# An order of units for each engine in the last two layers, and the output projection between two tiles of keys

## The reference

```
# third layer, x already normalised to xn
Q, K, V = split(xn @ W_in.T + b_in)
Q, K = rope(Q), rope(K)
A = sum over tokens of (K / |K|) * V
x = x + (A * Q) @ W_out.T + b_out + xn
# fourth layer, x normalised again to xn
hidden = sigmoid(xn @ ternary(w1).T) * (xn @ ternary(w2).T)
x = x + hidden @ ternary(w3).T
```

## Time and profile before

| what | us |
|---|---|
| median of 3 runs (lowest, highest) | 691.55 (690.04, 693.25) |
| the profiled execution, its time | 693.51 |
| its span in the profile | 691.7 |
| first combine of the last two layers starts at | 501.29 |
| the five steps with all five streams | 538.61 to 640.76 |
| last add of the last batch starts at | 688.35 |

### The profile page before, as it was taken

One profiled execution on the slowest core, in us unless ns is written; L12 is line 12 of the kernel. 1 busy time (PEld: TensorE's weight loads), 2 busy tenths in 40 slices (PEclk: granted clock), 3 DMA queues, 4 the chain that ended last, 5 costly groups with the idle time before them and its releaser, 6 DMA issues.

```text
span 691.7 us, 10447 instructions
## 1 busy us (share of the span) xinstructions
PE 529.4 (77%) x3558; PEld 429.6 (62%) x3558; DVE 404.3 (58%) x981; ACT 294.5 (43%) x617; POOL 281.5 (41%) x417
## 2 busy tenths in 40 slices
PE   3275878888898888888656569999246898888976
PEld 2143555656565665657445469899234888888876
DVE  2453455756676766665255358886146676776653
ACT  2405455563636464642411147555133443354432
POOL 3606060645536262620232423343366566544110
PEclk9656979998899999998986689999768999999998
DMA  8500000020200000100100383444611011100000
GB/s 318 211 0 18 2 16 16 2 62 2 60 2 32 17 33 16 33 17 16 31 31 1 91 292 99 112 115 108 206 46 31 31 46 46 47 17 1 16 16 30
DMA packets 31347, 39.56 MB, mean 57 GB/s; under 512 B 9632, under 2 KB 27552, under 8 KB 30400
## 3 DMA queue, kind: packets, MB, share of 16 engines
q1 hardware_dynamic: 26016, 25.31, 11.0%
q0 software_dynamic: 4432, 9.33, 5.3%
q10 hardware_dynamic: 848, 4.26, 1.6%
HBM read 27.25 MB, written 11.51 MB: 56 GB/s over the span
## 4 chain that ended last, share of the span: by engine, by line
PE 49%; DVE 19%; ACT 12%; DMA 7%; POOL 6%; issue 5%; ACTq 1%; another core or an unknown queue 1%; SPq 0%; DVEq 0%; POOLq 0%
PE bank_c L1390 5%; PE bank_s L1290 4%; DVE nmx L959 4%; ACT pT L738 3%; PE bank_p L1290 3%; PE bank_s L1421 3%; PE bank_c L1372 3%; PE bank_g L1294 2%; PE bank_c L1294 2%; DMA tb_x<-row_ids 2%; PE bank_g L1296 2%; PE bank_c L1676 2%; PE bank_g L1295 2%; PE bank_c L1296 2%; PE bank_c L1295 2%
## 5 line engine op out<-in xcount | busy, mean ns | idle before, releaser
L738 ACT ACTIVATE pT<-bank_s 128x512 f32<-128x512 f32 x128 | 69.5, 595 | 41.9 <-PE bank_s L1421 41.4
L959 DVE TENSOR_REDUCE nmx<-bank_c 128x2 f32<-128x512 f32 x80 | 55.1, 688 | 45.3 <-PE bank_c L1390 38.4
L492 POOL TENSOR_TENSOR rt<-raw,rope_sb 128x384 f32<-128x384 f32 x16 | 16.0, 1001 | 119.8 <-ACT raw L677 106.6
L593 POOL DMA_INDIRECT xt<-h_rows,tb_x x39 | 37.3, 955 | 66.1 <-DMA tb_x<-row_ids 53.0
L1390 PE MATMUL bank_c<-kT,qT 64*128 64x256 f32 x160 | 43.3, 353 | 24.8 <-DVE nmx L959 20.1
L1390 PEld LDWEIGHTS bank_c<-kT,qT 64*128 64x128 f32 x160 | 25.9, 203 | 49.6 <-DVE nmx L959 37.2
L1421 PE MATMUL bank_s<-qT,kT 64*128 64x512 f32 x128 | 38.5, 528 | 9.8 <-ACT pT L738 5.8
L900 DVE TENSOR_TENSOR mh_lo<-bank_s,mh_hi 128x512 fp32r<-128x512 f32 (+1 forms) x42 | 27.3, 651 | 30.4 <-ACT mh_hi L667 30.3
L602 POOL DMA_INDIRECT yg<-y_rows,row x32 | 31.4, 980 | 23.4 <-DMA y_rows<-yt 14.8
L1372 PE MATMUL bank_c<-pT,vv 128*32 128x256 f32 x512 | 37.0, 409 | 1.3 <-ACT pT L738 1.2
L577 POOL DMA_INDIRECT row_ids<-tok,pos x32 | 31.6, 987 | 9.2 <-issue 8.6
(11 more groups left out here) (303 smaller groups left out, 1785.2 us busy)
## 6 DMA issues: line engine op xcount, KB each, us to landing
y_rows<-yt SPq DMA_DIRECT2D x39, 128.0 KB, 2.4
we_raw<-in_w_e SPq DMA_DIRECT2D x4, 1216.0 KB, 13.7
xL<-in_x SPq DMA_DIRECT2D x8, 256.0 KB, 2.8
xW<-in_x SPq DMA_DIRECT2D x8, 256.0 KB, 2.7
h_rows<-hB SPq DMA_DIRECT2D x8, 256.0 KB
x_mid<-xW SPq DMA_DIRECT2D x8, 256.0 KB, 2.1
xB<-x_mid SPq DMA_DIRECT2D x8, 256.0 KB, 4.5
out_y<-xB SPq DMA_DIRECT2D x8, 256.0 KB, 2.1
```

The source lines that it names most:

```text
L738: ops.activation(probs(a, h, tc), bS[h], ACT.Exp).then_inc(a_exp, 1)
L959: ops.tensor_reduce(dst, first_bank(u).rearrange("p (st n) -> p st n", st=NT), AX.X, ALU.max, negate=True).then_inc(a_max, 1)
```

## The change

The shared string goes. Each engine gets its own, without empty slots, and `phase_b` takes only the streams that an engine has. The empty yields are removed from the generators. Three units are cut in two: on ScalarE tanh and take, on VectorE hd and sp, and combine and stats. On GpSimd `krn` and the query's rotation become two units, in the same order as before. No instruction is added or removed, and no semaphore changes. The new orders:

```diff
-PATTERN_B = "GFYGFKKYFNKKKNFFGK"
+ORDER_PE = "FYFKYKFKNFGK"
+ORDER_ACT = "FYFFGKFKFNFKNG"
+ORDER_DVE = "GGYFFFYFKFFKNFKG"
+ORDER_POOL = "GGYKKG"
...
-        def phase_b(*streams):
-            assert {c: PATTERN_B.count(c) for c in B_SLOTS} == B_SLOTS
-            stream = dict(zip(B_SLOTS, streams))
+        def phase_b(order, **streams):
             for step in range(BATCHES + 3):
-                live = {c: stream[c](step - lag) for c, lag in LAGS_B.items() if 0 <= step - lag < BATCHES}
-                for c in PATTERN_B:
+                live = {c: streams[c](step - lag) for c, lag in LAGS_B.items() if c in streams and 0 <= step - lag < BATCHES}
+                for c in order:
                     if c in live:
                         next(live[c])
...
                     ops.activation(fth[g % 2][:, :], hidden(g)[0], ACT.Tanh, scale=0.5).then_inc(f_th, 1)
+                    yield
                     take(fhd[g % 2][:, :], fT_hi[q][:, :], f_hd, g + 1, f_thi)
                     yield
...
                     dve.wait_ge(b_comb, at(b, 2, k + 1))
+                yield
                 stats("attn", x)
                 yield
-                yield
                 transposed(cT_hi[:, :], cT_lo[:, :])
...
                     ops.scalar_tensor_tensor(out=fhd[g % 2][:, :], in0=fth[g % 2][:, :], scalar=1.0, in1=hidden(g)[1], op0=ALU.add, op1=ALU.mult).then_inc(f_hd, 1)
+                    yield
                     split(fhd[g % 2][:, :], fT_hi[q][:, :], fT_lo[q][:, :], f_thi, g + 1, f_tlo)
                     yield
-                yield
...
```

More of the change, by code:

```diff
@@ L279, in build @@
         LAGS_B = {"G": 0, "K": 1, "Y": 2, "N": 2, "F": 3}
-        B_SLOTS = {"G": 3, "K": 6, "Y": 2, "N": 2, "F": 5}
         def phase_a(*streams):
@@ L297, in phase_m @@
                 pass
-        def phase_b(*streams):
-            assert {c: PATTERN_B.count(c) for c in B_SLOTS} == B_SLOTS
-            stream = dict(zip(B_SLOTS, streams))
+        def phase_b(order, **streams):
             for step in range(BATCHES + 3):
-                live = {c: stream[c](step - lag) for c, lag in LAGS_B.items() if 0 <= step - lag < BATCHES}
-                for c in PATTERN_B:
+                live = {c: streams[c](step - lag) for c, lag in LAGS_B.items() if c in streams and 0 <= step - lag < BATCHES}
+                for c in order:
                     if c in live:
                         next(live[c])
+                assert all(next(rest, False) is False for rest in live.values())
         def hT(buf, t):
@@ L630, in keys @@
             def keys(b):
-                for _ in range(3):
-                    yield
                 pool.wait_ge(b_ssm, b + 1)
                 ops.tensor_tensor(krn[:, :], ssm[:, :], mhalf[:, :], ALU.pow).then_inc(b_krn, 1)
+                yield
                 pool.wait_ge(b_qev, b + 1)
@@ L641, in keys @@
                 yield
-                yield
-                yield
             def mix(b):
-                yield
                 scale("ffn", b)
                 yield
[L650 to L658, removed]
+            phase_b(ORDER_POOL, G=results, K=keys, Y=mix)
         @block.scalar
@@ L855, in keys @@
                 ops.activation(qb[:, :], bC[0], ACT.Copy).then_inc(b_qev, 1)
-                for _ in range(4):
-                    yield
+                yield
             def mix(b):
                 transposed(yT_hi[:, :])
-                yield
                 yield
@@ L874, in feed @@
                     ops.activation(fth[g % 2][:, :], hidden(g)[0], ACT.Tanh, scale=0.5).then_inc(f_th, 1)
+                    yield
                     take(fhd[g % 2][:, :], fT_hi[q][:, :], f_hd, g + 1, f_thi)
                     yield
-                yield
-                yield
-            phase_b(results, keys, mix, norm, feed)
+            phase_b(ORDER_ACT, G=results, K=keys, Y=mix, N=norm, F=feed)
         @block.vector
@@ L1282, in feed @@
                 yield
-            phase_b(results, keys, mix, norm, feed)
+            phase_b(ORDER_DVE, G=results, K=keys, Y=mix, N=norm, F=feed)
         @block.tensor
@@ L1679, in feed @@
                 yield
-                yield
-            phase_b(results, keys, mix, norm, feed)
+            phase_b(ORDER_PE, G=results, K=keys, Y=mix, N=norm, F=feed)
 def fold(w):
```

## The result

The changed kernel takes 681.32 us (median of 4 runs, 678.99 to 683.19) beside 692.4 us of the kernel before (4 runs): a ratio of 0.9843, 95% interval 0.9802 to 0.9885, so 1.6% faster, which is 10.9 us by the ratio and 11.1 by the medians. I had forecast 678.0 against 691.55, 13.6 us. A second set of runs beside the later experiments gave 0.9808 (0.9744 to 0.9872).

The account below looks back on a forecast made before the run. The bound was taken as a loop over two engines' orders, not one engine. Gains of 11.35 (full steps), 0.95 (step 8), 0.3 (step 9) and 1.0 (step 2) total 13.6 us, giving a median of 678.0, range 671 to 686.

Parts of the forecast that it names:

- The full steps: Steps 3 to 7, with five streams, from F1 to F1: 18.0 us each instead of 20.43.
- The term of the five steps: Steps 3 to 7 together: 90.8 us against 102.15, a gain of 11.35.
- the first step: First full step: begins with TensorE below its full clock, some 0.8 us lost, so 18.8 us instead of 18.0.
- the N loop: Y2's result, VectorE's add and statistics, GpSimd's scale, ScalarE's Nnorm, N: 4.95 us from add to N, N at 13.15.
- term of about 0.2 for tanh2: ScalarE: tanh2 ends at 11.95, while Nnorm behind it would want to start at 11.68: 0.2 late.
- second hold of GpSimd: GpSimd's scale: first product meets sp1 on VectorE, the last may meet rot; 0.1 to 0.5 us added before N.
- price of 2.5 us over five steps: By the skill's exclusion rule, a second full GpSimd hold of 0.5 us per step, against the 1.5 or so taken.
- F4's new wait: TensorE between N and F4: take2 is behind Nnorm, so F4 waits for sp2, 0.8 us of new idle time.
- The clock: F4 in steps 4, 5 and 7: about 5 us of the 11.35 (1.5, 1.2, 1.6) no longer lost to low clock.
- The rival that the clock would go on falling in the full steps: F4 or what follows partly at 1.2 GHz: 6 to 7.5 us come back, 684 to 685.5; 682 to 688 has 0.18.
- Step 9: Step of 15.72 us: earlier yT and Y2, but F4 gets the same wait for take2; gain 0.3 us.
- The beginning: Steps 1 and 2: early Y2 takes 1.61 off N's wait, order yb, cT costs 0.6; gain 1.0 us.

Follow-up runs that it names:

- second set of runs beside the later experiments: The changed kernel, unaltered, run once more beside three of its variants; 0.9808 (0.9744 to 0.9872) of the time of the kernel before.
- early Y2 alone: Kernel before with only TensorE's new order (Y2 ahead of K2), ScalarE and VectorE keeping their old orders; 1.0004 (0.9975 to 1.0034).
- early add alone: Kernel before with only ScalarE's and VectorE's new orders and smaller units, TensorE keeping K2 ahead of Y2; 1.0043 (1.0011 to 1.0075).
- four variants of them: Changed kernel with take2 ahead of Nnorm (0.9825), F4's sp2 wait behind its first 8 matmuls (0.9735), extra matmuls in steps 9 and 10 (0.9786), both latter edits (0.9718).
- take2's swap: Changed kernel with take2 ahead of Nnorm again on ScalarE; 0.9825 (0.9784 to 0.9867) of the time of the kernel before.
- repeated profile: Profile of the changed kernel, unaltered, run once more beside three variants; ratio to the kernel before 0.9808 (0.9744 to 0.9872).
- three variants run beside it: Changed kernel with F4's sp2 wait behind its first 8 matmuls (0.9735), with extra matmuls in steps 9 and 10 (0.9786), with both edits (0.9718).
- filled kernel before: Kernel before with 16 extra matmuls of 256 columns on TensorE between K3 and N of each step with a batch in F; 0.9904 (0.9870 to 0.9938).
- filling the gap: Changed kernel with extra matmuls, 24 ahead of N in step 9 and 20 ahead of F4 in step 10; 0.9786 (0.9726 to 0.9846).

## Why the prediction was right

*The bound.* I took it to be the loop from Y2 over the add, the scale and Nnorm back to N, and not an engine. The experiments bear it out: the early Y2 alone and the early add alone leave the time at 1.0004 and 1.0043, both together give 0.984; at the full clock their steps are 20.59 and 19.58 us, together 17.93, where before it is 19.4. N came 13.02 us after F1; I had 13.15. In the changed kernel this loop no longer binds (see below). Which of the swaps on ScalarE and VectorE are needed was not run one by one.

*The full steps.* Forecast 18.0 us, measured 17.93 to 17.95 (18.07 for the first). The term of the five steps was 11.35 and came out as 12.33. Of the surplus of 0.98, 0.73 is the first step, which I had charged 0.8 us for a low clock; in this profile it ran at 1.00. That was luck: of six profiles with the new orders (first, repeated, and four variants of them) only this one and that of take2's swap ran it at the full clock. In the repeated profile its F1 took 3.57 us instead of 2.08 and the step 19.48, and in the three variants run beside it the first full step took 19.7 to 20.0. The five steps of the repeated profile took 91.21 us, a gain of 10.94.

*How the N loop came about.* From add to N it was 5.13 us, 4.95 before. The term of about 0.2 for tanh2 was right: the scale was done at 587.51, ScalarE had tanh2 until 587.99, and Nnorm followed directly behind it. The term of 0.1 to 0.5 for a second hold of GpSimd came out as nothing: the hold by sp1 is there (0.55 instead of 0.20), but the last product was no longer held, so one hold had moved and none was added, and the scale was 0.4 us ahead of ScalarE. N came 0.05 behind Nnorm's end, 0.18 later than K3 would have let it. The hold agrees with the Trainium skill (SBUF — State Buffer, Who interferes with whom) in the mechanism; the price of 2.5 us over five steps that the prediction worked out from it was not paid.

*F4's new wait.* Its place and size were right (0.8 forecast, 0.68 after the handover from N, 0.86 in start times). Its cause, as the prediction put it ("take2 is now behind Nnorm"), was wrong. The chain is F3's data, tanh2, hd2, take2, sp2; Nnorm fits into the time in which ScalarE waits for hd2. The swap back showed it: take2 no earlier (12.84 against 12.87 after F1), N 1.48 late, the step 0.65 longer. That the wait came out at the size that I had from a wrong cause is luck. With the old order on TensorE, Nnorm comes later and the cause is as I had it.

*The clock.* I expected about 5 us to come back; the three figures that I gave for it (1.5, 1.2, 1.6) add up to 4.3 only. The filled kernel before shows the clock on its own: its five full steps took 97.74 us, 4.4 less than before, 1.5 in each of steps 4, 5 and 7. So of the 12.33 about a third is clock, which 16 extra matmuls a step bring without any new order, and 7.9 are left, for the order and for the first step's clock. The rival that the clock would go on falling in the full steps did not happen: F4 was at 1.00 in every one, behind waits of 0.7 us. The waits that the page of the Trainium skill (TensorE: Matmul & The Clock Gate, HAM oscillation) has in its example are longer than the 2.3 us of the kernel before; that the clock falls behind 2.3 us is shown by these traces alone.

*Step 9 is the term that was mis-sized.* I forecast a gain of 0.3 us and it lost 1.40. N came 1.07 us earlier in the step (11.35 after F1 instead of 12.42), F4's new wait took back 0.93 of that, and F4 itself took 4.43 us instead of 2.89. So the order gained 0.14 there, and the low clock is the whole loss. TensorE idles 3.25 us ahead of this N (3.05 before). I had applied what the rows showed, that the clock may be low behind such an idle stretch, to the full steps and not to the ends. The repeated profile has the same (5.21 us), and filling the gap brings 2.88 and a step of 15.59. In the profile of before this F4 was at the full clock; with TensorE's order alone it had the same 3.05 us of idle time ahead of it and took 4.0. So the loss is also an accident of the one profile of before.

*The beginning.* Forecast 1.0, measured 1.28; Y1 waited for cT in step 1 as expected, A to Y1 being 2.69 us instead of 2.00, and N's wait in step 2 fell from 1.97 to 1.29. That the sum came so near is partly luck: the stretch from the first combine to step 3's F1 took 35.6 to 37.5 us in the six profiles whose kernels have all the new orders or differ by one swap or wait from them, and 37.3 and 37.6 in the two with all the old ones.

*The time.* 13.6 us forecast, 13.0 in the trace from the first combine on, 10.9 in the ratio. The difference between the last two is within the interval of the ratio (±2.9 us). The start of the last two layers lay between 497.0 and 506.6 us over the profiles of this study, with the same code ahead of it; that is as large as the effect, and is why the windows decide here and not one run's time.

## What to carry to other kernels

When several engines share one static order, look for the loop that goes through all of them, and time its edges on each engine: here two reorderings that are worth nothing alone (at the full clock they cost 1.2 and 0.15 us a step) gave 1.6% together, 1.5 us a step at the full clock. Moving work of another stream behind the producer (K2 behind Y2) pays only if the consumer's engine is free when the product arrives. Look at what follows TensorE's idle stretches, here of 2.3 to 3.3 us: a few useless matmuls in the gap made the kernel before 1.0% faster.

## What the runs showed of the hardware

TensorE's granted clock fell behind idle stretches in some steps and not in others with the same code: behind 2.3 us ahead of N in three of the four such steps of the kernel before, behind 1.66 us ahead of N and 0.68 ahead of F4 in three of six steps (ScalarE's and VectorE's orders alone), and behind 3.05 to 3.25 us ahead of N in six of seven profiles. Each time the F4 that followed took 4.0 to 5.2 us instead of 2.9. Behind 1.4 to 1.5 us it stayed at 2.4 GHz in all 14 F4s, and so it did with the stretch cut to 0.4 us by extra matmuls. A GpSimd product of 128x2 numbers, 0.20 us by itself, took 0.55 or 0.73 us when VectorE ran an operation of 512 columns with both inputs in SBUF, and ended some 0.05 us behind it; beside one of the same length with one input in PSUM it took 0.20.
